# Sandwich block on one core: the sum of the gelu values moves from TensorE to GpSimd, and the results after the FFN move to head 9

## What is computed

```
x = x + layernorm(attention(layernorm(x)))        # 16 heads of 32, causal, rotation by head
x = x + layernorm(ffn(x))

def bitlinear(x, w):                              # w has -g, 0 or +g only
    xn = (x - mean(x)) / sqrt(var(x) + 1e-6)
    return xn @ ternary(w).T                      # values are rounded to themselves
ffn(x) = bitlinear(gelu(bitlinear(x, w_fc)), w_down)   # 512 -> 2048 -> 512
```

## Time and profile before

| | |
|---|---|
| median of 3 runs | 1337.46 us (1334.47 to 1338.87) |
| the profiled execution | 1333.62 us |
| span from its first to its last instruction | 1331.8 us |
| mean granted clock of TensorE | 0.958 |
| busy: PE, DVE, ACT, POOL | 90%, 77%, 58%, 45% of the span |
| a usual iteration, from one up phase to the next (533.26 to 681.13) | 147.9 us |

### The profile page before, as it was taken

One profiled execution on the slowest core, in us unless ns is written; L12 is line 12 of the kernel. 1 busy time (PEld: TensorE's weight loads), 2 busy tenths in 40 slices (PEclk: granted clock), 3 DMA queues, 4 the chain that ended last, 5 costly groups with the idle time before them and its releaser, 6 DMA issues.

```text
span 1331.8 us, 24946 instructions
## 1 busy us (share of the span) xinstructions
PE 1192.1 (90%) x9364; PEld 648.4 (49%) x9364; DVE 1019.6 (77%) x2931; ACT 769.0 (58%) x1414; POOL 593.6 (45%) x636
## 2 busy tenths in 40 slices
PE   4755879999999999999999999999999999988796
PEld 2322545455545554455545554455545554554352
DVE  7588896878878797978788787968787887776532
ACT  3334874666556664666556754666466755576470
POOL 6131441692049502791159412871259313971252
PEclk9865898999999999999999999999999999999798
DMA  5451122002310113002300213002300221001000
GB/s 205 132 154 62 38 70 57 1 2 57 96 40 3 39 51 103 1 8 67 89 32 2 57 43 94 1 18 70 106 1 3 57 78 27 2 9 48 9 1 32
DMA packets 49825, 65.37 MB, mean 49 GB/s; under 512 B 8581, under 2 KB 33189, under 8 KB 49192
## 3 DMA queue, kind: packets, MB, share of 16 engines
q1 hardware_dynamic: 49704, 63.77, 16.5%
HBM read 29.89 MB, written 8.39 MB: 29 GB/s over the span
## 4 chain that ended last, share of the span: by engine, by line
PE 51%; DVE 33%; ACT 8%; POOL 3%; issue 3%; SPq 1%; DMA 1%; POOLq 0%; DVEq 0%; ACTq 0%
PE gen L488 18%; PE down L531 17%; DVE score L1089 9%; PE pv L585 4%; DVE hT L950 4%; PE score L557 4%; DVE probs L950 2%; DVE acc_add L1066 2%; PE score L563 2%; DVE mx L1089 1%; DVE qkn L1181 1%; POOL rstd L1422 1%; DVE bn L1118 1%; ACT qkn L753 1%; PE gen L548 1%
## 5 line engine op out<-in xcount | busy, mean ns | idle before, releaser
L1422 POOL TENSOR_TENSOR rstd<-veps,mhalf 128x1 f32<-128x1 f32 (+1 forms) x104 | 67.5, 649 | 472.5 <-DVE veps L1166 363.9
L809 ACT ACTIVATE probs<-score 128x512 f16<-128x512 f32 (+1 forms) x384 | 202.4, 527 | 122.1 <-PE score L557 122.1
L950 DVE TENSOR_TENSOR probs<-score,probs 128x512 f16<-128x512 f32 (+1 forms) x384 | 213.4, 597 | 61.2 <-ACT score L811 60.8
L488 PE MATMUL gen<-x2T,t1T 128*128 128x512 f16 x1024 | 242.6, 382 | 4.0 <-ACT x2T L752 2.5
L531 PE MATMUL down<-t2T,hT 128*128 128x512 f16 x1024 | 234.1, 381 | 3.5 <-DVE xn L1151 3.5
L811 ACT ACTIVATE score<-score 128x512 f32<-128x512 f32 (+1 forms) x384 | 205.4, 535 | 0.0
L488 PE MATMUL gen<-xT,wa 128*128 128x512 f16 x768 | 178.6, 383 | 12.2 <-DVE wa L970 8.4
L950 DVE TENSOR_TENSOR hT<-gen,hT 128x512 f16<-128x512 f32 x160 | 108.9, 687 | 65.8 <-ACT gen L772 27.6
L1089 DVE CUSTOM_DVE_ANT_0 score<-score,mask_rows 128x512 f32<-128x512 f32 (+1 forms) x344 | 158.0, 523 | 0.0
L531 PEld LDWEIGHTS down<-t2T,hT 128*128 128x128 f16 x1024 | 96.7, 98 | 111.3 <-DVE xn L1151 4.7
L488 PEld LDWEIGHTS gen<-x2T,t1T 128*128 128x128 f16 x1024 | 95.4, 98 | 109.4 <-ACT x2T L752 5.2
(11 more groups left out here) (136 smaller groups left out, 1838.3 us busy)
## 6 DMA issues: line engine op xcount, KB each, us to landing
qk<-qkn SPq DMA_DIRECT2D x384, 64.0 KB, 2.0
xo<-x SPq DMA_DIRECT2D x8, 1024.0 KB, 5.6
hT<-x SPq DMA_DIRECT2D x8, 1024.0 KB, 6.3
out<-xn SPq DMA_DIRECT2D x32, 256.0 KB, 2.2
hT<-w_fc SPq DMA_DIRECT2D x4, 1024.0 KB, 6.4
hT<-w_down SPq DMA_DIRECT2D x4, 1024.0 KB, 5.5
hT<-w_attn SPq DMA_DIRECT2D x4, 512.0 KB, 10.0
hT<-w_attn SPq DMA_DIRECT2D x1, 1024.0 KB, 8.7
```

Of the source, the lines that this page charges most:

```text
L488: mm = nc.tensor.matmul(bank[:, :], a, b, start=(start and n == 0), stop=(stop and n == len(pairs) - 1))
L809: nc.scalar.activation(probs[:, h % 2, HI, 512 * i:512 * i + n], score[i][:, 0:n], ACT.Exp, scale=1.0 / S_UP)
L950: return V.tensor_tensor(out, whole, hi, ALU.subtract)
```

## The change

`GpSimd` gets a fourth 128x512 operation for each block after the first: it adds `HI + LO` also to a new buffer `acc_sum`. In iterations 1 to 7 PE no longer runs `hidden_sums`; `square_sums` instead takes both `acc_sum` and `acc` over the partitions, 8 f32 matmuls instead of 4, ahead of `weigh(9)` instead of `weigh(6)`. `hidden_mean` and `hidden_variance` stand behind `probs_low(10)`, ahead of `head_output(9)`.

The first block is now drained by a plain copy (`drain(0)`), at its old place, and gets its mean subtracted later in place (`centre(0)`). At head 9 DVE does `final(1)`, `centre(0)` and the moments and terms of blocks 0 and 1 one after the other. The pieces of `ffn_down` for block 2 move from heads 9 and 10 to 11 and 12, those for block 3 from 13 and 14 to 14 and 15, and `final(2)` from head 12 to 13. Iteration 8 keeps its own path.

```diff
-DOWN_AT = {0: [(1, 0)], 5: [(1, 1), (1, 2)], 6: [(1, 3)], 9: [(2, 0), (2, 1)], 10: [(2, 2), (2, 3)],
-           13: [(3, 0), (3, 1)], 14: [(3, 2), (3, 3)]}
-FINAL_AT = {8: 1, 12: 2}
-SQUARES_AT = 6
-FINISH_AT = {6: 0, 9: 1, 13: 2}
+DOWN_AT = {0: [(1, 0)], 5: [(1, 1), (1, 2)], 6: [(1, 3)], 11: [(2, 0), (2, 1)], 12: [(2, 2), (2, 3)],
+           14: [(3, 0), (3, 1)], 15: [(3, 2), (3, 3)]}
+FINAL_AT = {13: 2}
+SQUARES_AT = 9
+FINISH_AT = {10: 0, 11: 1, 14: 2}
...
                     if prev:
-                        for tb in ((), (0, 1), (2,), (3,))[g]:
+                        for tb in ((), (0,), (1, 2), (3,))[g]:
                             store(tb)
...
                     pe.wait_ge(sq_step, SQ_STEPS * j if here else SQ_STEPS * (j - 1) + FC - 1)
-                    for tb in range(TB):
-                        mm = nc.tensor.matmul(pv[:, H_SQ + tb:H_SQ + tb + 1], acc[:, PARTS * tb:PARTS * (tb + 1)],
-                                              ones32[:, 0:1], start=True, stop=True)
+                    for at, of in ((H_SUM, acc_sum), (H_SQ, acc))[0 if here else 1:]:
+                        for tb in range(TB):
+                            mm = nc.tensor.matmul(pv[:, at + tb:at + tb + 1], of[:, PARTS * tb:PARTS * (tb + 1)],
+                                                  ones32[:, 0:1], start=True, stop=True)
...
                         up(u)
-                        if u >= 2:
+                        if u >= 2 and not here:
                             hidden_sums(u - 2)
...
+                def drain(tb):
+                    need(dve, stored[tb % 2], 16 * (2 * (j - 1) + tb // 2))
+                    dve.wait_ge(down_full, TB * (j - 1) + tb + 1)
+                    V.tensor_copy(xn[:, tb % 2, :], down[:, :]).then_inc(down_drained, 1)
+                def centre(tb):
+                    dve.wait_ge(down_drained, TB * (j - 1) + tb + 1)
+                    V.scalar_tensor_tensor(out=xn[:, tb % 2, :], in0=c_sum[:, :], scalar=h_negm[:, tb:tb + 1],
+                                           in1=xn[:, tb % 2, :], op0=ALU.mult, op1=ALU.add).then_inc(centred, 1)
...
                         if h + 1 < HEADS:
                             probs_low(h + 1)
+                        if prev and h == SQUARES_AT:
+                            hidden_mean()
+                            hidden_variance()
                         head_output(h)
+                    if prev and here and h == SQUARES_AT:
+                        final(1)
+                        centre(0)
+                        final_moments(0)
+                        final_terms(0)
+                        final_moments(1)
+                        final_terms(1)
...
+                        P.tensor_tensor(acc_add[:, :], hT[:, HI, u, :], hT[:, LO, u, :], ALU.add).then_inc(sq_step, 1)
+                        pool.wait_ge(sq_step, n + 1)
+                        P.tensor_tensor(acc_sum[:, :], acc_sum[:, :], acc_add[:, :], ALU.add).then_inc(sq_step, 1)
                         pool.wait_ge(sq_step, n + 2)
+                        P.tensor_tensor(acc_add[:, :], acc_add[:, :], acc_add[:, :], ALU.mult).then_inc(sq_step, 1)
+                        pool.wait_ge(sq_step, n + 3)
                         P.tensor_tensor(acc[:, :], acc[:, :], acc_add[:, :], ALU.add).then_inc(sq_step, 1)
```

More of the change, by code:

```diff
@@ L199, in build @@
         acc_add = sb("acc_add", [PARTS, T], f32)
+        acc_sum = sb("acc_sum", [PARTS, T], f32)
         oA = sb("oA", [PARTS, 2, TB, HD], f32)
@@ L528, in ffn_down @@
                         need(pe, down_drained, TB * (j - 1) + tb)
+                    if tb == 0 and here:
+                        drained("up", 4 * part + 3)
                     for u in range(4 * part, 4 * part + 4):
@@ L668, in iteration @@
                     ffn_down(0, 1)
-                    hidden_sums(FC - 2)
-                    hidden_sums(FC - 1)
+                    if not here:
+                        hidden_sums(FC - 2)
+                        hidden_sums(FC - 1)
                 if here:
@@ L1125, in hidden_mean @@
                 def hidden_mean():
[L1126 to L1128 removed]
+                    if here:
+                        dve.wait_ge(pv_full, HEADS * j + SQUARES_AT + 1)
+                    else:
+                        dve.wait_ge(hsum_full, 1)
+                    dve.wait_ge(hsq_full, j)
                     V.tensor_scalar(h_negm[:, :], pv[:, H_SUM:H_SUM + TB], -1.0 / F, None, ALU.mult
```

43 lines of the change are left out of this document (20 added, 23 removed).

## The result

The change takes 1426.8 us (1425.6 to 1427.3, 4 runs) against 1337.3 us (1334.5 to 1338.9, 4 runs), a ratio of 1.067 [1.065, 1.069]: 6.7% slower. The forecast was 1408 us, its range ended at 1426. Direction and mechanism held; 19 us of the loss were not in the sum. The profiled execution took 1427.3 us with a span of 1425.5 us; the span stands 93.7 us above that of before (1331.8), where the sum had 74.

The account below looks back on a forecast made before the run. PE and DVE were taken to hold the bound by turns. 54.6 us for six usual iterations, 7.6 for iteration 7 and 11.9 for the clock made 74 us on top of 1333.6: 1408 us, range 1382 to 1426.

Parts of the forecast that it names:

- The up phase: Ahead of the heads, per iteration: 0.8 us less from removed sums, 1.0 us more from the later power for next x.
- POOL's end and the squares: Usual iterations: POOL ends at 619.4 us, PE reaches head 9 at 621.5; 2 us of cover left, no cost.
- rival 3: POOL bounds every iteration, its new addition costing 1.7 us instead of 1.37: 18 us more, 1426 us; chance 0.12.
- Iteration 7: At head 9 PE and DVE stand still 10 us for POOL's last sum; 7.6 us more, without the clock's term.
- The main mechanism: Heads 8 to 15: moved `ffn_down` pieces and DVE's block at head 9 make the last weighing 8.9 us later.
- Rival 4: PE runs ahead into head 11, filling idle time of heads 9 and 10: 28 us more, 1362 us; chance 0.07.
- Rival 1: Moved work finds cover in heads 11 to 15, only removals count: 14 us less, 1320 us; chance 0.06.
- the clock's term: PE idles 3.9 us between heads 10 and 11, clock falls: 1.7 us in each of seven iterations, 11.9 us.
- the walk: Step-by-step times of PE and DVE through heads 8 to 15: last weighing starts at 662.9 us against 653.95.
- Rival 2: The clock stays up despite the gap between heads 10 and 11: 1396 us; chance 0.25.
- head 11: PE's start there waits for head 10's first maximum, behind DVE's block: 631.2 us against 630.21, 1.0 us more.
- head 14: PE starts at 652.0 us, takes 3.45, 0.2 waiting, 0.77, 0.4 waiting and 0.6, and ends at 656.9.

Follow-up runs that it names:

- The late pieces alone: Kernel before with only the block 2 and 3 pieces of `ffn_down` at heads 11, 12, 14, 15 and `final(2)` at head 13: 1389.2 us, 1.040.
- the filled run: Kernel before with only the pieces moved late, plus 32 useless matmuls at the start of heads 9 and 10 in the six usual iterations: 1382.3 us, 1.034.
- With the idle filled: The change plus useless matmuls in iterations 1 to 6, 32 ahead of head 9 and 60 ahead of head 11's product: 1404.6 us, 1.050.
- pieces back: The change with block 1 also drained by plain copy and the pieces back at heads 9, 10, 13, 14; POOL's sums stay: 1360.2 us, 1.016.
- the additions alone: Kernel before plus GpSimd's additional addition in groups 1 to 6 only, its result unread: 1347.4 us, 1.008.
- the last version: Kernel before with only the seventh iteration on the change's late places, TensorE sums, no plain copies: 1334.0 us against 1337.6, 0.998.

## Why the prediction was right or wrong

**Right, by the rows and the runs.**

- *The up phase.* Forecast -0.8 + 1.0 = +0.2 us up to `scores(0)`; measured -0.1. Alone, the removed sums are worth 1.2 and the first six of fifteen additions cost 0.7.
- *POOL's end and the squares.* 619.4 forecast, 619.1 measured, so rival 3 was out in the usual iterations. Iteration 7 was to stand still for 10 us and stood for 13; its 9.3 us (clock included) measured 10.4. The runs give it as 13.8 for the standstill less 3.3 for the late places, which without it bring the iteration to 129.3 us.
- *The main mechanism*: the two pairs of pieces moved out of idle PE time onto the path. 7.9 us were forecast for heads 11 to 15. The late pieces alone cost 10.0 by the profiles, and about 7.2 in the two iterations of the filled run in which the clock never fell.
- *PE's place in the order.* Rival 4 (PE runs ahead into head 11) is out: the product waits for the maximum, as the row at 661.53 says. Rival 1 is out by its own condition: heads 11 and 12 needed 3.5 us of idle PE time each, and PE waits 0.31 us at head 12 in the change as before.

**Wrong: the clock's term.** "I add 1.7 us to each of the seven", from one gap and one fall. That gap of 3.9 us was placed between heads 10 and 11. But the walk itself had PE wait for the freed banks at head 9, and gave that wait no clock. In the trace the clock is down from there on, comes back in four of six iterations to fall once more around the start of head 11, and falls again at head 13; the gap ahead of head 11 is 2.6 to 3.2 us. Two falls were the upper end, 3.5 us. The price of a single fall was right (1.4 to 1.8 us in the runs), the number of falls was not: the clock misses 6.8 or 10.2 us in a usual iteration instead of 1.7. With the idle filled the usual iteration is 3.3 us shorter, twice the term. Rival 2 (the clock stays up) goes the other way from what was found.

The trace of before could have warned of it. The prediction takes the gap of 2.80 us in the earlier trace rows as its model, but 35 us earlier in the same iteration the clock had fallen behind a shorter one:

```profile
1193.89 0.61 PE L563 MATMUL score<-mask_b,identb 128*128 128x512 bf16 x1 [1.51 <-DVE probs L950]
```
```profile
1194.00:1196.00 2.00, 2.00 (x20) 1.47 (x20) 1.90 (x5) 1.83 (x4) 1.07 (x2) 0.50 0.00 0
```

**Wrong by the same step: head 11.** Forecast +1.0 us; measured +3.1 in iterations 3 and 6, +2.1 to +2.6 in the others. The block itself has the forecast length. But the sums (1.71 and 1.84 us instead of 1.0 each) and the weighing ahead of it ran at half clock, and DVE waited 0.76 + 0.89 us for them. So the half clock was not only a loss of PE's own time, as priced, but was on DVE's path too, which the block ends. With the idle filled head 11 is +1.5 to +1.6 in five of six iterations, so 0.5 us of the error has another cause.

One sum of the walk is short by itself: head 14 from 652.0 us with 3.45, 0.2, 0.77, 0.4 and 0.6 ends at 657.4, not 656.9.

**The balance** of a usual iteration: forecast 10.8 us, measured 13.8. From the runs: sums -1.2, additions +0.7 (six of fifteen), late pieces +10.0, DVE's block and the sums at head 9 +3.1 (pieces back, 2.6, less the two first terms), and 1.2 that exist only together, 0.3 of them in the up phase. Six times the 3.0 missing are 18.1 of the 19.6 us between 93.7 and 74.1; the seventh iteration has 1.1, the two ends of the program 0.4. The forecast stood on the profiled execution of before, 3.8 us under the median; from the median it would have been 1411 us, still 15 short.

On the rules: the Trainium skill (TensorE: Matmul & The Clock Gate, "What's actually happening") has two states, the fast one held by activity; the run of the late pieces with the idle filled agrees: 32 useless matmuls each at heads 9 and 10 keep 1.00 where the clock was 0.50. The rule of the Trainium skill on the port that DVE and POOL share (SBUF — State Buffer, "SBUF: two separate sides") bears on the additions. The trace of the additions alone doesn't show it: ACT's wait of 1.78 us for the late `shift` stands beside 0.1 us more of work on DVE. No run here tests the rule at `xo`.

**Open:** why iterations 3 and 6 stay at half clock longer than the others; why the same wait of 2.00 us at head 13 is followed by a fall in some iterations and not in others; where the 0.2% of the last version come from.

## What to carry to other kernels

Work that stood in a bound engine's idle time was free there and cost its full length elsewhere (two pairs of pieces, 3.45 us of PE each, cost about 7.2 us an iteration at full clock): before moving a matmul, look at what its place was filling. A gap on TensorE cost more than its length here; every instruction up to the clock's return is slower, and whoever waits for those waits longer, so walk the clock through all gaps, not the largest alone, and search the trace of before for the shortest gap behind which it fell. And price an iteration of another shape (the last one) by itself: a cover of 2 us in six iterations was a wait of 13 in the seventh.

## What the runs showed of the hardware that was not expected

Short gaps were enough to bring the granted clock down: 2.0 us ahead of the row at 648.6 us in the change, 2.2 us ahead of the one at 639.8 in the run of the late pieces, 1.5 us at 1193.9 in the trace of before. But a gap of that length did not always do it: the same 2.00 us at head 13 were followed by 0.50 in all six usual iterations of the change, in four of six with the late pieces and filled idle time, and in three of six of the change with filled idle time. A single fall cost 1.4 to 1.8 us. With 32 and 60 matmuls of zeros the same code ran 22 us faster, and with 64 in the kernel with late pieces alone 7 us faster.
